# One attention kernel, five edits: gathers of values moved, one more split head, buffers moved, waits moved, operands on 64-byte addresses

## The reference, cut to what matters

```python
x = x + _L0_cond_ref(x, L0_cond_weights, itok_B_0_15)          # 32x32 map per batch
x = x + _L1_cond_ref(x, itok_B_0_15, L1_cond_weight)           # 512x512 map per batch
x = x + _L2_cond_ref(x, itok_B_0_31, L2_cond_weights, L2_cond_biases)
...
q, k, v = x @ Wq.T, x @ Wk.T, x @ Wv.T       # 32 query heads, 8 key heads, D = 128
q, k = rope(rmsnorm(q)), rope(rmsnorm(k))
k_all = concat(k_cache[block_table], k)      # 16 pages of 32 keys, and 32 new keys
v_all = concat(v_cache[block_table], v)
scores = where(valid, q @ k_all.T * SCALE, -1e30)
o = softmax(scores) @ v_all
x = x + o @ Wo.T
```

## Time and profile before

| | us |
|---|---|
| three runs | 2285.64, 2288.32, 2289.05 (median 2288.32) |
| the profiled execution | 2286.66 |
| its span | 2284.8 |
| TensorE busy | 2231.2 (98%) |
| VectorE busy | 1675.9 (73%) |
| ScalarE busy | 1297.7 (57%) |
| GpSimd busy | 1137.8 (50%) |

### The profile page before, as it was taken

The page is one execution under the profiler, slowest core; times in us unless marked ns, Lnnn a source line. Parts: engine busy times, 40 slices in busy tenths (PEclk is TensorE's granted clock), DMA queues, the critical chain, the costliest instruction groups (busy, mean ns, idle before and its releaser), DMA issues. The chain is left out here.

```text
span 2284.8 us, 52315 instructions
## 1 busy us (share of the span) xinstructions
PE 2231.2 (98%) x16384; PEld 1935.1 (85%) x16384; DVE 1675.9 (73%) x3504; ACT 1297.7 (57%) x2643; POOL 1137.8 (50%) x1218
## 2 busy tenths in 40 slices
PE   7998999999998999999999999999999998999999
PEld 6777777777776999999999999999999997888887
DVE  7860788888887888888888888888888886422221
ACT  6732888888886555555555555555555555311111
POOL 5200354544445777777777777777777773000000
PEclk9999999999998999999999999999999999999999
DMA  6643243444347888888888888888888885543442
GB/s 263 217 107 92 86 127 114 132 134 127 116 140 244 302 303 300 299 297 300 297 290 289 292 297 299 298 301 295 302 300 292 300 298 188 188 139 105 121 129 64
DMA packets 451816, 501.70 MB, mean 220 GB/s; under 512 B 95863, under 2 KB 390775, under 8 KB 443416
## 3 DMA queue, kind: packets, MB, share of 16 engines
q1 hardware_dynamic: 414872, 366.44, 49.3%
q0 software_dynamic: 36864, 134.23, 16.6%
HBM read 408.21 MB, written 92.34 MB: 219 GB/s over the span
## 5 line engine op out<-in xcount | busy, mean ns | idle before, releaser
L1192 POOL TENSOR_TENSOR att_probs<-att_probs,att_inverse 128x512 f32<-128x512 f32 x512 | 535.9, 1047 | 255.0 <-DVE att_inverse L1402 250.7
L1300 ACT ACTIVATE att_probs<-att_probs,att_low 128x544 f32<-128x544 f32 x512 | 383.7, 749 | 472.9 <-DVE att_low L1389 472.9
L1256 PE MATMUL att_o<-att_probs_t,att_values 128*128 128x128 f32 x4096 | 541.0, 275 | 2.1 <-DMA att_values<-L_cond_v_cache,att_v_rows_of 1.8
L1256 PEld LDWEIGHTS att_o<-att_probs_t,att_values 128*128 128x128 f32 x4096 | 497.6, 192 | 2.5 <-DMA att_values<-L_cond_v_cache,att_v_rows_of 2.0
L1389 DVE CUSTOM_DVE_ANT_0 att_probs<-att_score,att_mask,att_batch_cols 128x544 f32<-128x544 f32 x512 | 400.6, 782 | 129.2 <-PE att_score L1218 84.6
L1398 DVE COPY att_probs_t<-att_turn 128x512 f32<-128x512 f32 x512 | 351.0, 686 | 1.2 <-PE att_turn L1233 1.2
L1178 POOL DMA_INDIRECT att_values<-L_cond_v_cache,att_v_rows_of x256 | 270.8, 1058 | 82.5 <-POOL att_v_rows_of L1174 50.1
L1233 PE MATMUL att_turn<-ident,att_probs 128*128 128x128 f32 x2048 | 310.1, 274 | 0.8 <-POOL att_probs L1192 0.4
L1005 POOL TENSOR_TENSOR proj_q_out<-proj_by_cos,proj_by_sin 128x512 f32<-128x512 f32 x128 | 188.6, 1474 | 216.8 <-DVE proj_by_sin L931 216.8
L1233 PEld LDWEIGHTS att_turn<-ident,att_probs 128*128 128x128 f32 x2048 | 241.9, 141 | 36.2 <-issue 8.8
L862 PE MATMUL proj_proj<-x3t_hi,proj_w_hi 128*128 128x512 f32 x640 | 254.6, 398 | 6.7 <-DVE proj_w_lo L916 6.7
(11 more groups left out here) (156 smaller groups left out, 4101.1 us busy)
## 6 DMA issues: line engine op xcount, KB each, us to landing
keys_first<-L_cond_k_cache SPq DMA_DIRECT2D x512, 128.0 KB
att_keys_raw<-L_cond_k_cache SPq DMA_DIRECT2D x512, 128.0 KB
q_t<-proj_q_out SPq DMA_DIRECT2D x32, 1024.0 KB, 5.4
o_t<-att_heads_out SPq DMA_DIRECT2D x64, 512.0 KB, 6.6
out_o_raw<-o_t SPq DMA_DIRECT2D x31, 1024.0 KB, 5.3
queries_first<-q_t SPq DMA_DIRECT2D x32, 512.0 KB
att_queries_raw<-q_t SPq DMA_DIRECT2D x32, 512.0 KB
maps_even<-L_cond_weight SPq DMA_DIRECT2D x8, 1024.0 KB, 12.3
```

Of the source, the lines that this page charges most:

```text
L1192: nc.gpsimd.tensor_tensor(probs[:, k, 0:L], probs[:, k, 0:L], inverse[:, k:k + 1].to_broadcast([P, L]), ALU.mult).then_inc(probs_ready, 1)
L1256: last = nc.tensor.matmul(o_ps[:, at:at + P], values[j][:, t, h * D:(h + 1) * D], probs_t[m % 2][:, t * P:(t + 1) * P], start=(t == 0 and ...
L1300: nc.scalar.activation(probs[:, k, :], probs[:, k, :], ACT.Exp, bias=low[k][:, 0:1], scale=-1.0, accum_out=total[k][:, 0:1]).then_inc(exp_ ...
```

## The change

Five things, in one diff. (1) `NATIVE` goes from 4 to 3: five heads of a batch use split keys and queries, the parts grow by a quarter, and ScalarE and VectorE start with them one head earlier. (2) The gathers stand in the slots of heads 3, 5 and 7 of the batch before, and the fourth in the batch's own head 0. (3) `w_hi0`, `w_lo0`, `keys_first`, `queries_first`, `o0_hi` and `o0_lo` move to the top of the memory, above 19696 floats that the stages fill from below; the first head's projection weights are split in the first stage, ScalarE's part behind the copies of group 9, VectorE's at its end. (4) SP no longer waits for the stores of the values at the end of the first stage; GpSimd waits for them before its first addition in the second. SP's wait for the stored keys moves from the third stage to the end of the second. (5) Eight floats are put in ahead of two runs of buffers, and 384 ahead of `wot0_hi`, so that those buffers begin at multiples of 64 bytes.

```diff
+BELOW_HIGH = 19696
 def stage_maps_values(...):
+    V_AT = 5120
+        a_.sb("to_64_bytes", [P, 8])
         with nc.sbuf_tensor("maps_even", [P, CONDS, IC, P], F32) as even:
...
-            for u in range(U):
-                sp.wait_ge(v_stored[u], 16 * GB * (G // U))
-            sp.wait_ge(w_nat_loaded, 32)
...
                 then(nc_v.tensor_scalar(rope[:, n, :], src, wcol[:, w:w + 1], None, ALU.mult))
+            for m in range(1 + REP):
+                dve.wait_ge(w_hi_ready, m + 1)
+                nc_v.tensor_tensor(w_first_lo[:, m].rearrange("p c e -> p (c e)"), w_nat[:, m, :],
+                                   f32(w_first_hi[:, m]).rearrange("p c e -> p (c e)"), ALU.subtract).then_inc(w_ready, 1)
...
             for g in range(2, 10):
                 keep_values(g)
+            act.wait_ge(l1_groups, 4 * UNITS)
+            act.wait_ge(w_nat_loaded, 32)
+            for m in range(1 + REP):
+                copy(w_first_hi[:, m].rearrange("p c e -> p (c e)"), w_nat[:, m, :]).then_inc(w_hi_ready, 1)
             act.wait_ge(reduced, 2)
 def stage_projection(...):
...
             heads(sp, head)
+            for rc in range(RC):
+                sp.wait_ge(k_stored[rc], 16 * HK)
...
-            for m in range(M):
-                split_weights(0, 0, m, True)
             heads(act, head)
...
             nc.gpsimd.memset(ones[:], 1.0).then_inc(ones_ready, 1)
+            for u in range(2):
+                pool.wait_ge(v_stored[u], 16 * GB * (G // 2))
             heads(pool, head)
 def stage_attention(...):
-    NATIVE = 4
-    ACT_FROM, DVE_FROM = 4, 5
+    NATIVE = 3
+    ACT_FROM, DVE_FROM = 3, 4
...
-    FIRST_ACT = {0: (1, 2), 1: (3, 4), 2: (5,)}
-    FIRST_DVE = {0: (0,), 1: (1, 2), 2: (3, 4), 3: (5,)}
+    FIRST_ACT = {0: (1, 2), 1: (3, 4, 5)}
+    FIRST_DVE = {0: (0,), 1: (1, 2), 2: (3, 4, 5)}
...
+        a_.sb("to_64_bytes", [P, 8])
         new_probs_t = [a_.sb(f"new_probs_t{n}", [P, P]) for n in range(2)]
         heads_out = [a_.sb(f"heads_out{v}", [P, HK, P]) for v in range(2)]
+        a_.sb("foot", [P, 384])
         wot0_hi = a_.sb("wot0_hi", [P, REP, HID], F32R)
...
-            for rc in range(RC):
-                sp.wait_ge(k_stored[rc], 16 * HK)
...
-                    if 3 <= h < 3 + PPT and not (last_pair and j == 1):
+                    if h == 0 and (j or not first):
+                        load(j, i * 2 + j, PPT - 1)
+                    if h in (3, 5, 7) and not (last_pair and j == 1):
                         if h == 3 and (j or not first):
                             pool.wait_ge(o_done, i * N + j * HK)
-                        load((j + 1) % 2, i * 2 + (j + 1), h - 3)
+                        load((j + 1) % 2, i * 2 + (j + 1), (h - 3) // 2)
 def program(...):
+                with nc.sbuf_tensor("below_high", [P, BELOW_HIGH], F32):
+                    with (nc.sbuf_tensor("w_hi0", [P, 1 + REP, IC, P], F32R) as w_hi0,
+                          nc.sbuf_tensor("w_lo0", [P, 1 + REP, IC, P], F32R) as w_lo0):
+                        pass
+                    with (nc.sbuf_tensor("keys_first", [P, NPP + 1, HK, PSIZE], F32) as keys_first,
+                          nc.sbuf_tensor("queries_first", [P, HK, P], F32) as queries_first):
+                        pass
+                    with (nc.sbuf_tensor("o0_hi", [P, REP, CB, S], F32R) as o0_hi,
+                          nc.sbuf_tensor("o0_lo", [P, REP, CB, S], F32R) as o0_lo):
+                        pass
```

More of the change, by code:

```diff
@@ L90, in stage_maps_values @@
 def stage_maps_values(nc, x, weight1, cond, subj, w0, w2, bias2, wv, wq, wk, table, seqlens, freq, qw, kw, ident,
-                      early, x3t_hi, x3t_lo, rope, w_nat, stat, v_index, x3_dram, vn_dram):
+                      early, x3t_hi, x3t_lo, rope, w_nat, stat, v_index, x3_dram, vn_dram, w_first, w_sems, v_stored):
     QUADS = G // 4
@@ L117, in stage_maps_values @@
     BY_POOL = (((), (), (), ()), ((), (3,), (), ()))
+    w_first_hi, w_first_lo = w_first
+    w_hi_ready, w_ready = w_sems
+    V_AT = 5120
     with ExitStack() as ctx:
@@ L155, in stage_maps_values @@
         adapters = [even, odd.rearrange("p (a c o) -> p a c o", a=CONDS, c=IC)]
-        v_out = [odd[:, u * KVD:(u + 1) * KVD].rearrange("p (q h d) -> p q h d", q=GB, d=D) for u in range(U)]
-        pages = odd[:, U * KVD:U * KVD + B * NPP].bitcast(I32).rearrange("p (b n) -> p b n", b=B)
+        v_out = [odd[:, V_AT + u * KVD:V_AT + (u + 1) * KVD].rearrange("p (q h d) -> p q h d", q=GB, d=D) for u in range(U)]
+        pages = odd[:, 0:B * NPP].bitcast(I32).rearrange("p (b n) -> p b n", b=B)
         l1_ps, l2_ps, turn_ps = banks[2:4], banks[4:6], banks[6:8]
@@ L718, in stage_projection @@
         SCALE_AT = {9: 0, 12: 1, 14: 2, 16: 3}
[L720 to L725, removed]
+        w_hi = [w_first[0], a_.sb("w_hi1", [P, M, IC, P], F32R)]
+        w_lo = [w_first[1], a_.sb("w_lo1", [P, M, IC, P], F32R)]
+        w_hi_ready, w_ready = w_sems
         ones = a_.sb("ones", [P, S])
@@ L733, in stage_projection @@
         stat_t = a_.sb("stat_t", [P, CB, S])
+        k_out = [a_.sb(f"k_out{n}", [P, CB, S]) for n in range(RC)]
         q_out = [a_.sb(f"q_out{n}", [P, CB, REP, S]) for n in range(2)]
-        k_out = [a_.sb(f"k_out{n}", [P, CB, S]) for n in range(RC)]
         proj_ps = [a_.ps(f"proj{k}") for k in range(RING)]
@@ L874, in _, with split_weights @@
         def _(act):
-            def split_weights(h, u, m, first=False):
-                if m == 0 and not first:
+            def split_weights(h, u, m):
+                if m == 0:
                     act.wait_ge(w_loaded, h * 32)
@@ L975, in head @@
                         scale_k(h, SCALE_AT[t])
-            for m in range(M):
-                split_weights(0, 0, m)
             dve.wait_ge(first_pages_loaded, 16)
@@ L1014, in stage_attention @@
                     keys_first, queries_first, first_pages, keys_loaded, q_stored, k_stored,
[L1015 removed]
+                    wo, w_nat, out_sems, o_first):
     wo_loaded, wo_hi_ready, wo_ready, o_loaded, o_hi_ready, o_lo_ready, o_stored = out_sems
@@ L1464, in stage_output @@
         y = [a_.sb(f"y_rows{v}", [P, HID]) for v in range(2)]
+        wot_hi = a_.sb("wot_hi", [P, HQ - REP, HID], F32R)
+        wot_lo = a_.sb("wot_lo", [P, HQ - REP, HID], F32R)
         y_ps = [a_.ps(f"y{g}") for g in range(GC)]
@@ L1674, in program @@
         k_stored = [ctx.enter_context(nc.semaphore(f"k_stored{rc}")) for rc in range(RC)]
+        v_stored = [ctx.enter_context(nc.semaphore(f"v_stored{u}")) for u in range(2)]
+        w_hi_ready = ctx.enter_context(nc.semaphore("w_hi_ready"))
+        w_ready = ctx.enter_context(nc.semaphore("w_ready"))
+        w_sems = (w_hi_ready, w_ready)
         wo_loaded = [ctx.enter_context(nc.semaphore(f"wo_loaded{v}")) for v in range(2)]
@@ L1687, in program @@
                   nc.sbuf_tensor("rope", [P, 4, ROWS], F32) as rope):
+                with nc.sbuf_tensor("below_high", [P, BELOW_HIGH], F32):
[8 more added lines that the diff above has]
+                        pass
                 stage_maps_values(nc, x, w1, cond, subj, w0, w2, b2, wv, wq, wk, table, seqlens, freq, qw, kw, ident,
[L1689 to L1693, removed]
+                                  early, x3t_hi, x3t_lo, rope, w_nat, stat, v_index, x3_dram, vn_dram, (w_hi0, w_lo0), w_sems, v_stored)
                 stage_projection(nc, wq, wk, ident, x3t_hi, x3t_lo, rope, w_nat, stat, qt_dram, kn_dram, k_inv_dram, table, kc,
-                                 keys_first, queries_first, first_pages, first_pages_ready, keys_loaded, q_stored, k_stored)
+                                 keys_first, queries_first, first_pages, first_pages_ready, keys_loaded, q_stored, k_stored,
+                                 (w_hi0, w_lo0), w_sems, v_stored)
             first_head = stage_attention(nc, table, vc, ident, stat, v_index, kc, kn_dram, qt_dram, vn_dram, ot_dram,
                             keys_first, queries_first, first_pages, keys_loaded, q_stored, k_stored,
-                                         wo, w_nat, out_sems)
+                                         wo, w_nat, out_sems, (o0_hi, o0_lo))
         stage_output(nc, wo, ident, ot_dram, x3_dram, out.rearrange("b s t -> (b s) t"), w_nat, first_head, out_sems)
```

13 lines of the change are left out of this document (3 added, 10 removed).

## The result

The changed kernel takes 2329.95 us (median of 4 runs, 2328.83 to 2335.87); the kernel before took 2287.08 beside it. The ratio is 1.0192, 95% interval 1.0173 to 1.0212: slower by 43 us, where 21 us less were forecast. One of e11's five executions took 5407 us and is left out of its figures.

| us | before | after | difference |
|---|---|---|---|
| to the end of the values | 222.07 | 218.58 | -3.5 |
| gap to the first projection matmul | 6.74 | 3.51 | -3.2 |
| projection, to the first score matmul | 491.80 | 495.23 | +3.4 |
| attention, to the first output matmul | 1203.51 | 1256.10 | +52.6 |
| output | 360.7 | 360.6 | -0.1 |

A forecast was written before the change was run, and what follows sets the result against it. TensorE, busy for all of a steady 18.46 us attention batch, was taken as the bound. Gains of 10.2 + 1.5 + 3.0 + 3.1 + 2.3 + 1.0 = 21.1 us from 2286.7 gave 2266 us, range 2254 to 2286.

The forecast's parts named there:

- the fourth gather: Attention, batch's own head 0: lands 3.4 to 6.9 us after its descriptors, taken as 4 with 5.1 available; cost nothing.
- last gather comes late: Rival, attention: first product of every batch waits for the gather; 2381 us at 6.9 us landing, 2330 at 6.1; chance 0.09.
- five split heads: Attention: one of eight heads goes from native to split, 0.16 us a batch over 64 batches, 10.2 us less.
- The rival on VectorE: Attention: VectorE becomes the bound in split heads; 2277 us, or 2286 to 2297 with 0.3 us lost a batch; chance 0.16.
- Gathers spread: Attention: spacing the four gathers lets GpSimd catch up, so the 0.40 us split block mostly goes; 1.5 us less.
- the rival that gathers do the same: Attention, heads 5 and 7: a gather holds the port and blocks VectorE's split, next mask late; 2356 us, chance 0.06.
- Values to projection: Gap between values and projection: the store wait and most of the weight split go, 3.0 us less, bounds 1.8 to 4.
- Values operands: Values stage: 64-byte alignment speeds 384 matmuls by 5.3 to 10 ns each; 2.3 us less.
- Output operands: Output stage: 64-byte alignment saves 5.3 ns on each of 576 matmuls of heads 2, 4 and 6; 3.1 us less.
- Small products and slots: Small products with new_probs_t and the adapter slots: alignment gives 0 to 4 us, taken as 1.0 us less.

The follow-up runs named there:

- e11: e5 with the three high buffers at a multiple of 256 bytes instead of 64; 2276.88 us, ratio 0.9957.
- e1: The changed kernel with its four gathers put back into heads 3, 4, 5 and 6 of the batch before; 2321.69 us, ratio 1.0152.
- e4: The changed kernel with every second page's key load bringing 8 of 128 partitions from the third batch on; 2294.83 us, ratio 1.0033.
- e9: The changed kernel with gathers in heads 3, 4, 5, 7 and ScalarE multiplying heads 4 and 6 except 8 of 512 columns; 2269.91 us, ratio 0.9923.
- e5: The changed kernel with gathers back in heads 3 to 6, as e1, and four split heads again; 2279.86 us, ratio 0.9973.
- e10: The changed kernel with gathers in heads 3 to 6 and ScalarE multiplying heads 4 to 6 except 8 of 512 columns; 2278.58 us, ratio 0.9963.

## Why the prediction was wrong

The step that failed is the fourth gather: "So 3.4 to 6.9 us; I take 4 [...] and cost it at nothing". In the 52 batches that waited it took 5.1 to 7.6 us (median 5.9) from descriptors to use, against 4.7 or 5.3 available. The rival "last gather comes late", with its point of decision at 5.4 us and its 2330 for 6.1 us, describes the result; it was given 0.09. That its number is the measured one is partly luck: it stands for 64 us of waits on top of all gains, and the run has 43 us of waits and not the fifth head's gain. The reason for taking 4, "only one other gather is still under way", looked at the wrong queue: what stood ahead was SP's loads, and before's own packets by queue put the landing at 5 to 6 us.

A second step failed with it, and would have been enough alone: *five split heads*, 10.2 us less, with 1.4 us of VectorE's time "spare" and 1.0 of it known to lie in one place. The rival on VectorE had the mechanism, but as one that the spread gathers take away. They moved it: from the splits of heads 5 to 7 to that of the queries in head 1. And VectorE's time was not the only one short: with the gathers in four successive heads GpSimd needs 2.4 us a head and TensorE waits for its multiplies (e1). e4, without the gather's wait, is at 2294.83, e1, with the gathers back, at 2321.69, both slower than before (e4 by 0.3%). The term itself was right where nothing holds VectorE up: e9's attention is 11.8 us shorter than e5's, though e9 feeds the heads otherwise too. *Gathers spread*, 1.5 less, is part of the same: it can't be had apart from the fourth gather.
The Trainium skill (SBUF — State Buffer, "SBUF: two separate sides") has it that a VectorE instruction with two SBUF inputs and a GpSimd one that reads SBUF exclude each other for the whole length of the one that began first. The prediction left out the condition that it reads SBUF, and no run shows whether a gather meets it. The 1.16 beside 0.65 in e1 agrees for multiplies; the rival that gathers do the same did not come about: 65 of e9's smaller splits began while a gather ran and took 0.65 in the median, their time alone.

The small terms stand. *Values to projection*: 3.2 for 3.0. *Values operands*: 233.6 to 227.1 ns, 384 times: 2.5 for 2.3. *Output operands*: 233.3 to 228.9 for 576 matmuls, 2.5, less 0.3 for the first head's (227.2 to 228.9), 2.2 for 3.1; e1 and e5 show 358.1 and 358.4 for before's 360.7. In the profiled execution of after the clock took it back: behind a wait of 2.7 us the output's stretch 1987 to 1992 had 0.68 on the mean, where before, behind 2.3 us, had 1.00. *Small products and slots*, 1.0, can't be told: the values end between 216.8 and 220.8 in kernels whose first stage is the same.

Three costs were not in the sum. The first head's weights came to lie 192 bytes off the rows that they multiply: 231.4 for 229.6 ns, 960 times, 1.7 us. TensorE's clock is at its lower level (0.50, 1.2 GHz) behind the gap, for 4.0 us in before and 5.4 in after; in e10 it isn't, and there the projection, with the same places, takes 491.8 us for 495.2. Windows of after, behind the gap and behind the output's wait (the number behind the busy times is the granted clock):

```profile
222.10:227.30 5.20, 5.20 (x12) 4.11 (x13) 0.17 (x1) 0.00 (x0) 0.00 (x0) 0.50 0.83 282
1987.00:1992.00 5.00, 4.62 (x14) 3.71 (x15) 2.29 (x5) 2.19 (x4) 0.00 (x0) 0.68 1.05 321
```

and the same of before:

```profile
228.80:232.40 3.60, 3.59 (x9) 2.82 (x10) 2.35 (x5) 1.22 (x3) 0.00 (x0) 0.50 0.10 9
1937.00:1942.00 5.00, 4.44 (x20) 3.69 (x21) 2.91 (x5) 3.13 (x5) 0.00 (x0) 1.00 1.00 329
```

And the first batch has its first split head one slot sooner, where TensorE now waits 3.0 us for the split queries.

## What to carry to other kernels

Here gathers of one size landed, in the median, 3.0 to 7.1 us behind their descriptors, by what the queues held ahead of them: before a transfer is moved towards its use, read in the trace when its own packets moved, queue by queue, not how long one of its kind took elsewhere. An engine's spare time counts only in the slot where the work is put, and one that shares a lock with another has less of it than its busy share says; where two such costs overlap, the one left can hold the time up (e4), so take both away before judging. Work that one engine can't place was worth moving to an idle third: two of eight multiplies on ScalarE, with the gathers in heads 3, 4, 5 and 7, turned the fifth split head from 42 us of loss (e5 to e1) into 10 of gain (e5 to e9).

## What was not expected of the hardware

The pace of 512-column matmuls depends on where the stationary and the moving operand begin relative to each other, modulo 256 bytes:

| apart | output, ns | projection and values, ns |
|---|---|---|
| 0 | 226.6 to 227.2 | 229.6 (values 227.1) |
| 192 | 228.9 | 231.4 |
| 128 | 232.4 | 234.5 |
| 224 | 233.3 | 233.6 (values) |

Each is read from one kernel or more, and e11's 0 was forecast from the others. It is the distance and not an address: before's first head had both operands 224 bytes past a multiple of 256 and ran at 227.2. In the 224 row the stationary operand is ahead in the output, the moving one in the values. The Trainium skill (TensorE: Matmul & The Clock Gate, "What happens when you issue a matmul") has weights and streaming operand on independent ports; up to 6.7 ns of 227 by their relative place is an effect that ports with nothing in common wouldn't show.
